# Reordering the start of a fused attention and expert kernel: level tables, value weights and the first unit

## The reference, cut to what matters

```
x = x + attn(layernorm(x));  x = x + ffn(layernorm(x))        # x: 8 sequences x 1024 tokens x 128
attn: q, k, v per head (8 heads of 128);  g = -softplus(x Wg + bg);  G = cumsum(g)
      lam = softplus(x Wdl + Lparam)                            # 12 levels for each head and token
      A[t, s] = (q_t . k_s) * scale * exp(G_t - G_s) * lam[t, level(t - s)]   for s <= t
      out = layernorm(concat(A v) Wo + x) * ln_g + ln_b
ffn:  softmax gate over 8 experts, best 2 kept and rescaled, weighted sum of (x We_e + be_e)
```

## Time and profile before

| | |
|---|---|
| median of 3 runs | 1462.64 us (1460.75 to 1463.16) |
| the profiled execution | 1460.58 us, span 1458.8 us |
| busy: PE, PEld | 1390.9 us (95%), 1166.3 us (80%) |
| busy: DVE, ACT, POOL | 1041.8 us (71%), 1157.7 us (79%), 933.1 us (64%) |
| mean granted TensorE clock | 0.993 |

### The profile page before, as it was taken

One profiled execution on the slowest core, in us unless ns is written; L12 is line 12 of the kernel. 1 busy time (PEld: TensorE's weight loads), 2 busy tenths in 40 slices (PEclk: granted clock), 3 DMA queues, 4 the chain that ended last, 5 costly groups with the idle time before them and its releaser, 6 DMA issues.

```text
span 1458.8 us, 30735 instructions
## 1 busy us (share of the span) xinstructions
PE 1390.9 (95%) x10478; PEld 1166.3 (80%) x10478; DVE 1041.8 (71%) x2445; ACT 1157.7 (79%) x3412; POOL 933.1 (64%) x1018
## 2 busy tenths in 40 slices
PE   5899999999999999999999999999999999999997
PEld 5687888878878788887888788887887878878875
DVE  4767666797767877687766976668776796667667
ACT  3789888887889778897788877889778987877742
POOL 2355569655696567955588556974569655696573
PEclk9999999999999999999999999999999999999998
DMA  5311111111211122011121011110211011111100
GB/s 190 72 18 18 31 19 32 18 23 40 40 9 17 24 40 40 18 11 38 25 40 14 17 34 23 39 18 18 45 24 23 17 24 26 39 18 19 24 8 15
DMA packets 256342, 44.05 MB, mean 30 GB/s; under 512 B 197960, under 2 KB 254522, under 8 KB 256058
## 3 DMA queue, kind: packets, MB, share of 16 engines
q1 hardware_dynamic: 253980, 41.69, 15.1%
q10 hardware_dynamic: 2206, 0.40, 0.2%
HBM read 32.31 MB, written 9.18 MB: 28 GB/s over the span
## 4 chain that ended last, share of the span: by engine, by line
PE 56%; POOL 18%; DVE 11%; ACT 9%; issue 3%; SPq 1%; DMA 0%; ACTq 0%; POOLq 0%; DVEq 0%
PE o_ps L1429 15%; POOL a_lo L615 9%; PE l_ps L1366 7%; PE s_ps L1345 5%; PE s_ps L1347 5%; PE s_ps L1346 5%; ACT w_all L769 5%; PE aux L1345 4%; PE aux L1347 4%; PE aux L1346 4%; DVE a_all L988 3%; ACT a_hi L791 2%; DVE z L1064 2%; POOL late L640 2%; POOL e_rs L621 2%
## 5 line engine op out<-in xcount | busy, mean ns | idle before, releaser
L615 POOL TENSOR_TENSOR a_lo<-a_all,a_hi 128x512 fp32r<-128x512 f32 (+2 forms) x640 | 719.4, 1139 | 476.8 <-ACT a_hi L791 474.6
L769 ACT ACTIVATE w_all<-l_ps,bias 128x128 f32<-128x128 f32 x2287 | 624.4, 388 | 22.5 <-PE l_ps L1366 21.0
L988 DVE TENSOR_TENSOR a_all<-s_ps,w_all 128x512 f32<-128x512 f32 (+3 forms) x768 | 419.7, 553 | 259.7 <-PE s_ps L1347 219.5
L791 ACT ACTIVATE a_hi<-a_all 128x512 fp32r<-128x512 f32 (+2 forms) x640 | 359.7, 595 | 196.1 <-DVE a_all L988 194.9
L1429 PE MATMUL o_ps<-a_hi,v_all 128*128 128x512 f32 (+2 forms) x1280 | 463.4, 367 | 11.1 <-POOL a_lo L615 11.1
L1429 PEld LDWEIGHTS o_ps<-a_hi,v_all 128*128 128x128 f32 x1280 | 240.8, 188 | 49.0 <-POOL a_lo L615 11.8
L1345 PE MATMUL s_ps<-q_hi,xt_hi 128*128 128x512 f32 (+2 forms) x640 | 258.6, 404 | 7.8 <-DVE a_all L988 7.0
L1347 PE MATMUL s_ps<-q_hi,xt_lo 128*128 128x512 f32 (+2 forms) x640 | 230.9, 361 | 0.0
L1346 PE MATMUL s_ps<-q_lo,xt_hi 128*128 128x512 f32 (+2 forms) x640 | 230.5, 360 | 0.0
L1429 PE MATMUL o_ps<-a_lo,v_all 128*128 128x512 f32 (+2 forms) x640 | 229.5, 359 | 0.0
L1366 PE MATMUL l_ps<-rb,mask 96*128 96x64 f16 (+1 forms) x1774 | 143.9, 221 | 11.4 <-ACT w_all L769 11.2
(11 more groups left out here) (234 smaller groups left out, 2118.7 us busy)
## 6 DMA issues: line engine op xcount, KB each, us to landing
rb<-eb_scratch SPq DMA_DIRECT2D x1016, 0.8 KB
ra<-ea_scratch SPq DMA_DIRECT2D x508, 4.0 KB, 2.0
mt<-m_scratch SPq DMA_DIRECT2D x62, 128.0 KB, 2.1
nt<-n_scratch SPq DMA_DIRECT2D x62, 128.0 KB, 2.6
tx<-in_L_attn_x SPq DMA_DIRECT2D x9, 512.0 KB, 4.2
out<-late SPq DMA_DIRECT2D x15, 256.0 KB, 2.8
late<-in_L_attn_x SPq DMA_DIRECT2D x7, 512.0 KB, 4.2
ea_scratch<-tx SPq DMA_DIRECT2D x15, 128.0 KB
```

Of the source, the lines that this page charges most:

```text
L615: pool.tensor_tensor(a_lo[r][:, 0:t1 - t0], a[r][:, 0:t1 - t0], a_hi[r][:, 0:t1 - t0].bitcast(F32), ALU.subtract).then_inc(a_lo_done, 1)
L769: last = act.activation(w[k][:, W_AT[j] + dd, :].rearrange("p (f c) -> p f c", f=2), l_tiles[:, :, :, i - i0], ACT.Exp, bias=bias[b % 2][: ...
L791: act.activation(a_hi[r][:, 0:t1 - t0], a[r][:, 0:t1 - t0], ACT.Copy).then_inc(a_hi_done, 1)
L988: dve.tensor_tensor(a[(n * NG + g) % NA][:, 0:t1 - t0], s_ps[:, g % 2, 0:t1 - t0], w[n % 2][:, at:at + (t1 - t0) // P, :].rearrange("p i n ...
```

## The change

SP loads the tables of head 0 before nt, and rb of head 1 right behind its ra, ahead of the x of sequence 1 and of the store of the value weights. TensorE runs unit(0, 0) before value pieces 0 and 1, and pieces 2 and 3 one unit later. No instruction is added or taken away.

```
                 sp.wait_ge(t["el_lo"], 2)
                 store_el_part(sp, 0, 1)
-                sp.wait_ge(s_hi, 2)
-                sp.wait_ge(s_lo, 2)
-                first_n()
                 sp.wait_ge(t["stored"], EL)
                 sp.wait_ge(zeroed, 4)
                 load_ra(sp, 0, range(TA // 2))
                 load_rb(sp, 0, range(HALF_B, TB))
+                sp.wait_ge(s_hi, 2)
+                sp.wait_ge(s_lo, 2)
+                first_n()
                 load_ra(sp, 1, range(TA))
+                load_rb(sp, 1, range(TB))
                 load_x(1)
                 store_weights(1)
                 sp.wait_ge(s_mst, 16)
-                load_rb(sp, 1, range(TB))
                 load_m(2)
...
                 keep_busy(s_ps[:, 1, :], 7)
-                for u in range(2):
-                    value(0, u)
                 for u in range(NU):
                     unit(0, u)
                     if u == 0:
+                        for k in range(2):
+                            value(0, k)
                         turn_expert_weights()
-                    if u < 2:
-                        value(0, u + 2)
+                    if u in (1, 2):
+                        value(0, u + 1)
                     if u in (2, 3):
                         scores(0, u - 2)
```

## The result

Ten runs of each kernel, in turn on one chip: 1465.74 us after (1464.51 to 1466.89) against 1461.82 before (1460.75 to 1463.16), a ratio of 1.0025 with a 95% interval of 1.0016 to 1.0035. The change makes the kernel 3.7 us slower (2.3 to 5.1). The profiled execution after took 1464.51 us (span 1462.7), 3.9 above the one before.

What follows compares the result with a forecast made beforehand. TensorE sets the loop's pace and VectorE the loop's start at 55.15. A shift of 4.0 us (3.5 at full clock) less 0.41 gave 3.1 to 3.7, taken as +3.5: 1466.1 us against the median 1462.64, range 1461.8 to 1468.4.

Steps and rivals of the forecast that it cites:

- SP's order: SP's queue before the loop: twelve table loads first, value weights at 42.5 instead of 37.75, first value piece at 46.1.
- VectorE: VectorE before the loop: idles 4.1 us (3.5 at full clock) for value piece 0; first weighed tile 59.2 instead of 55.15.
- What is given back: At unit(1, 1) the 1.64 us rb wait goes, but ScalarE's rest lets only 0.41 us count at unit(1, 2).
- The bound from GpSimd: GpSimd's low part for value product (0, 7) comes 4.0 late, so the shift is at least 3.7 us (3.2).
- The sum: The whole kernel: 3.1 to 3.7 us slower, taken as +3.5; 1466.1 us against the median of three runs.
- my own line of 2.9 us: For the kernel's time: a difference over 0.2%, 2.9 us, counts as faster or slower.
- Part 2: TensorE's order before the loop: unit(0, 0) ahead of value pieces 0 and 1, near 41.6 instead of 43.57, gives nothing.
- Cheap issues: Rival on SP's queue: twelve loads pass within 1.0 us, value weights hardly late, faster by up to 1.6 us; chance 0.05.
- Absorbed by the removed wait: Rival at unit(1, 2): ScalarE makes up its lateness, all 1.64 us counts, 2.4 slower (1.9 at full clock); chance 0.25.
- More is late: Rival: half clock lasts over unit(0, 1) and the turning, or head 2's tables come late; 4.5 to 5.5 slower; chance 0.10.

Runs made afterwards that it cites:

- e9_rb_back: The changed kernel with rb of head 1 put back behind the second x and the weights' store; 1465.28 us against 1460.99 before, ratio 1.0026.
- e1_rb_only: The kernel before with only the rb loads of head 1 moved ahead of the second x and the store; 1462.60 us against 1461.77, ratio 0.9997.
- e5_fold_early: The changed kernel with VectorE's folding of the expert weights ahead of its wait for the query weights; 1464.39 us against 1461.25 before, ratio 1.0017.
- e7_nt_later: The changed kernel with the value weights issued later still, behind head 1's eight ra loads; 1468.13 us against 1461.25 before, ratio 1.0042.
- e3_queue_only: The kernel before with only SP's order changed, both parts, and TensorE's order the old one; 1466.00 us against 1461.77, ratio 1.0021.
- e8_direct_fold: The changed kernel with TensorE's old order, first value pieces reading n_two without copy, folding in VectorE's earlier rest; 1460.66 us against 1461.25 before, ratio 0.9988.
- e6_nt_direct: The changed kernel with the first pair's value pieces reading n_two, without the copy to nt; 1461.05 us against 1461.25 before, ratio 0.9990.

## Why the prediction was right

**SP's order.** The start with ScalarE's queue, 37.45, came at 37.71 in an execution that was 0.24 later as a whole; the value weights at 42.5 came at 42.45, the first value piece at 46.1 came at 45.83 with a wait of 3.8. Nearly exact, since each term was a row, and in part by luck: SP started 0.26 later than forecast, its twelve issues took 4.64 instead of 4.97, and the 0.2 us by which TensorE started sooner behind the issue (3.38, not 3.58) went into the first piece (1.65 us to VectorE's copy, not 1.5).

**VectorE.** Forecast: a rest of 4.1 at the half clock (3.5 at the full), first copy at 47.6, first weighed tile at 59.2. Measured: 3.69, 47.48 and 59.16. The clock was half, as taken. The rest is 0.4 smaller than forecast because VectorE was free 0.29 later (43.79, not 43.5; the execution was 0.24 later as a whole) and the copy came 0.12 sooner. The two experiments that take this wait away and double it bear the step out: A moves by -3.7 and +4.4.

**What is given back.** I forecast 0.41 of the 1.64; the table says 0.50 (B from 7.33 to 6.83), in every kernel without the wait. It is the lateness itself that gives it back and not the move of rb, as e9_rb_back shows. The mechanism was right, and its place was half wrong: I let ScalarE hold TensorE at unit(1, 2) only. After, TensorE also waits 1.05 us at unit(1, 1), for the exponentials of unit(1, 0), which end at 62.7. I had read the bracket of the earlier trace rows as if the DMA were all that unit(1, 1) waited for; the row names the last to come only, and ScalarE, the second last, would have held the unit for the first 1.05 of the 1.64 us. The bound from GpSimd, at least 3.7, held where I had put it (3.74 at value product (0, 7)) but is no bound on the time: unit(2, 0) was 3.57 later.

**The sum.** Forecast 3.6, taken as 3.5. In the traces 28.07 - 24.80 = 3.27, and the remaining 0.6 of the 3.9 between the spans is 0.24 ahead of this stretch and 0.4 behind it, both within what changes from run to run. By the ratio it is 3.7. Against the median of three runs shown, 1462.64, I gave 1466.1; the median was 1465.74. Two errors cancel in this: the median before was 0.8 lower in ten runs than in three, and by medians the loss is 3.9. That the change counts as slower by my own line of 2.9 us is narrow as well; the interval, 2.3 to 5.1, holds the line.

**Part 2.** "This gives nothing" was wrong as a statement on unit(0, 0). Measured alone it costs 1.46 us, as its tables then come behind the value weights and the value pieces behind it run at the half clock; with the value weights late it saves 0.9 to 1.3 in the trace, as it fills a wait and takes itself out from between the value pieces and the turning of the expert weights. My term for the change as a whole was not touched by this, since I had derived the order as it was changed and not the difference that the order makes.

**The rivals.** Cheap issues: 12 of them took 4.64 us after (37.71 to 42.35), so out. Absorbed by the removed wait (2.4): out by the trace, 0.50 was given back, as e1_rb_only and e9_rb_back show on both sides; by the time alone it is not, as 2.4 lies just inside the interval. More is late: the half clock ended before unit(0, 1) in this execution and VectorE waited once; the late tables of head 2 (67.04 to 73.2 on SP's queue) held nobody. In e9_rb_back, e5_fold_early and e7_nt_later, where the half clock lasted to unit(0, 1), VectorE did not wait before the expert weights, and from its first copy to the first weighed tile it took 0.2 to 0.4 longer than after. So that part of the rival could come by chance, but at less than the 0.5 to 1 that I gave it; 1.0 us of such waits came only in e3_queue_only, with unit(0, 0) in the way.

## What to carry to other kernels

Before moving an item ahead in a queue of DMA issues, count the issues it is moved past and multiply: here twelve small table loads pushed two copies of 128 KB back by 4.7 us, while the wait that the change was to remove was worth 0.5. The price of a wait is not its length but the distance to the next engine that would have held the same instruction; read that engine's end before spending anything on it. And where a copy stands on the path only to put data in another place, look whether the consumer can read it where it is: that took 3.7 us off the changed kernel's first stretch, and with two moves of work into rests it made the only version whose time lies clear of before's, by a hair (0.9978 to 0.9998).

## What the runs showed of the hardware

In the stretch before, an issue on SP's queue took 0.31 to 0.56 us for a load of 4.0 KB (ra) and 0.30 to 0.74 for one of 0.8 KB (rb). Two queues issuing side by side (SP and ACT, 37.7 to 42.4 after) did not slow each other by a measurable amount: SP's four ra loads took 1.81 us and its eight rb loads 2.79, which is 0.45 and 0.35 each, and with ACT's queue at rest its next eight and sixteen took 4.07 and 5.61, 0.51 and 0.35 each. TensorE read its moving operand in two separate blocks of 128 (n_two) at the same pace as from a packed tile: starts 0.12 us apart at the full clock in e8_direct_fold, 0.21 at the half in e6_nt_direct, as for nt. And the stretch from unit(1, 2) to the end took 1395.8 to 1399.4 us in twelve executions of twelve kernels with the same instructions in it, with no order by what stood ahead of it: a difference of 1 us in a prologue has to be read in the trace, since the medians here can't resolve it.
